# Keys of a cross-attention turned by transposing DMAs instead of TensorE transposes

## The chip, the cores and the metric

The kernel runs on one core of a Trainium2 chip. The metric is the device time of one execution in microseconds, as the median of several runs. The core has TensorE (PE: matmuls and transposes), VectorE (DVE), ScalarE (ACT), GpSimd (POOL) and the sync engine's queue (SP), which only issues DMAs. All DMAs of the core share 16 DMA engines.

## The reference

Eight sequences of 256 tokens with 1024 features go through one cross-attention with a residual and one gated feed-forward network with a residual. Only the first part is touched by the change.

```python
def xattn(text, features, Wq, bq, Wk, bk):      # text: layernorm(x), features: ctx_4096 (8, 256, 1024)
    Q = jnp.einsum('btx,dx->btd', text, Wq) + bq
    K = jnp.einsum('bpx,dx->bpd', features, Wk) + bk
    scores = jnp.einsum('btd,bpd->btp', Q, K) / sqrt(1024)
    return jnp.einsum('btp,bpd->btd', softmax(scores), features)

x = x + xattn(layernorm(x), ctx_4096, Wq, bq, Wk, bk)
x = x + ffn(layernorm(x), gate_q, gate_absmax, up_q, up_absmax, down_q, down_absmax)   # 4-bit weights, 1024 -> 3584 -> 1024
```

## The kernel before

A preparation of about 110 us forms the product `A` of the two weight matrices, so that the scores need only `x A ctx^T` and rows of biases. Then come eight steps, one per sequence ("batch" `b`, functions named `step(b)` on each engine), of about 37 to 41 us each. After them the feed-forward network runs for about 1500 us.

To keep precision, every operand is held as a pair of fp16 numbers, high and low ("hi" and "lo"); a product is three matmuls (`PARTS`: hi hi, hi lo, lo hi). "Keys" are the 256 rows of `ctx` of one sequence. They are needed in two forms: in rows (`keys16`, for the weighted sum at the end of attention) and turned, features in partitions (`keysT`, moving operand of the scores).

One step in the order of each engine's program, which is written out by hand:

- TensorE: eight blocks `o = 0..7` of 24 matmuls (L1533) that form `R = A^T x^T`; after block 1 the probabilities of the sequence before are turned (L1478); after blocks 4 to 7 one quarter of the keys is turned each (`turn_keys`, four fp32 transposes by the identity, L1470). Then the quarters of the next sequence's x (`turn_x`, also L1470) stand between the matmuls of the weighted sum of the sequence before (`attended`, L1494). Last come 48 matmuls of scores (L1569), in two halves of which the first is split 15 + 9 by the last `turn_x`. Each step begins by waiting until all four quarters of its x are split on VectorE (`s_xlo`, L1760).
- ScalarE: evicts each R block twice (L1662, L1664), makes the normalised x (L1612), scales the keys to fp16 hi rows and to fp32 rows (`keys_hi`, L1618 and L1619, after blocks 2 and 3), evicts each turned quarter of keys as hi (`turned_keys_hi`, L1624), and those of x (L1603).
- VectorE: scales, layernorm statistics of a sequence two steps back, `keys_lo` (L1784: turned keys minus their hi part), then `x_lo(b + 1, 0..2)` (L1760) with residuals between (L1824), `key_max(b + 1)` (L1765: largest key, once the keys of the next sequence have landed), `x_lo(b + 1, 3)`, and the softmax's maximum (L1798).
- GpSimd: R's low parts (L1423, one per block), the low parts of the key rows (L1427, after blocks 3 and 4; they raise `s_klo`), differences for a Strassen-like form of the feed-forward input (L1183 to L1191), and at the end of the step `reduce_max(b + 1)` (L1415, L1416), a maximum over partitions that waits for `key_max(b + 1)`.
- SP queue, in order: pieces of decoded weights and loads of packed weights where a table puts them (`units_due`, L301 and L284), a prefetch of x (L1370), x rows for the residual (L1380), turns of feed-forward input by transposing DMAs (`t_turn`, L1228) with the store of an earlier one (`t_store`, L1239), the load of the next sequence's keys (L1389; it waits for `s_klo` of this sequence since the buffer `keys` is single), and the store of y (L1358).

So keys run through a ring over two steps: load (L1389), `key_max` on VectorE, `reduce_max` on GpSimd, `keys_hi` on ScalarE, key low parts on GpSimd, and then the load of the next keys.

## Time and profile before

| what | value |
|---|---|
| median of 3 runs | 1978.07 us (1976.69 to 1984.44) |
| span of the profiled execution, first to last instruction | 1973.9 us; no whole time of its own is given for it, and the median of the runs lies 4.2 us above the span |
| PE, DVE, ACT, POOL busy over the span | 98%, 83%, 75%, 20% |
| attention steps b = 1 to 7 | 152.77 to 420.20 us |
| DMA queue of SP: share of the 16 engines over the span | 35.2% |

"Busy" is the time in which an engine's instruction ran. A wait is put down to the instruction that released it. The granted clock is TensorE's, as a part of full speed. A DMA's landing is counted from the start of its issue.

### The profile page before, as it was taken

How to read it: one execution, taken by the hardware profiler on the slowest of the kernel's cores; microseconds unless marked ns; L12 is line 12 of the kernel's file. 1: busy time of each engine (PE TensorE's matmuls, PEld its weight loads, DVE VectorE, ACT ScalarE, POOL GpSimd, SP SyncE). 2: the span in 40 equal slices, each digit the busy share in tenths (PEclk: the TensorE clock that was granted, in tenths of full speed). 3: DMA queues.
4: the chain of work that ended last, by engine and by line, in shares of the span. 5: the costliest groups of instructions: out<-in, count | busy, mean ns of one | idle time of the engine just before them, and what ended most of it. 6: DMA issues, size and time to landing. Idle time of an engine off the chain costs nothing.

```text
span 1973.9 us, 29877 instructions
## 1 busy us (share of the span) xinstructions
PE 1928.0 (98%) x9872; PEld 983.3 (50%) x9872; DVE 1637.0 (83%) x2758; ACT 1484.2 (75%) x2758; POOL 404.3 (20%) x600
## 2 busy tenths in 40 slices
PE   8989999989999999999999999999999999999999
PEld 3468878754444444444444444444444444444444
DVE  6757888986988988988988998898898898996963
ACT  3767886757889889889889889889899999900000
POOL 0022464441211211211211211111123222201110
PEclk9999999999999999999999999999999999999999
DMA  9112689683555555554544644645569899893562
GB/s 346 30 49 65 170 233 233 180 299 72 140 127 119 148 125 124 148 130 113 156 122 117 156 127 113 150 129 120 137 176 239 230 216 247 217 274 117 173 224 85
DMA packets 393626, 314.63 MB, mean 159 GB/s; under 512 B 327296, under 2 KB 327296, under 8 KB 391552
## 3 DMA queue, kind: packets, MB, share of 16 engines
q1 hardware_dynamic: 347360, 159.07, 35.2%
q0 software_dynamic: 44032, 153.65, 23.9%
q8 instruction: 78, 1.28, 0.3%
q14 instruction: 76, 0.62, 0.1%
q10 hardware_dynamic: 2080, 0.01, 0.1%
HBM read 154.31 MB, written 82.31 MB: 120 GB/s over the span
## 4 chain that ended last, share of the span: by engine, by line
PE 53%; ACT 22%; DVE 12%; issue 6%; DMA 1%; DVEq 0%; ACTq 0%; POOL 0%
PE ps L2125 38%; PE ps L2167 12%; ACT sq L346 7%; ACT sq L342 5%; ACT w L346 2%; DVE w L362 2%; ACT w L342 2%; PE ps L1494 1%; ACT halves L414 1%; PE ps L1569 1%; DVE tail L2277 1%; ACT tail L2198 1%; ACT T L1664 1%; PE ps L1533 1%; DVE tail L1219 1%
## 5 line engine op out<-in xcount | busy, mean ns | idle before, releaser
L2125 PE MATMUL ps<-T,wS 128*128 128x512 f16 x4704 | 1017.6, 379 | 4.1 <-DVE ps L2232 2.5
L2125 PEld LDWEIGHTS ps<-T,wS 128*128 128x128 f16 x4704 | 459.8, 98 | 558.4 <-issue 4.9
L346 ACT ACTIVATE sq<-sq 128x512 f32<-128x512 f32 x898 | 516.2, 627 | 0.0
L362 DVE SCALAR_TENSOR_TENSOR w<-sq,w 128x512 f32<-128x512 f32 x590 | 417.3, 707 | 109.5 <-ACT sq L346 99.6
L342 ACT ACTIVATE sq<-q 128x512 f32<-128x512 int32 x598 | 362.9, 631 | 49.6 <-DVE w L362 47.5
L2167 PE MATMUL ps<-T,tail 128*128 128x512 f16 x1584 | 345.0, 379 | 5.3 <-issue 2.1
L2167 PEld LDWEIGHTS ps<-T,tail 128*128 128x128 f16 x1584 | 154.6, 98 | 193.3 <-issue 5.9
L1533 PE MATMUL ps<-T 128*128 128x256 f16 x1536 | 174.1, 273 | 4.2 <-DVE T L1760 4.1
L2167 PE MATMUL ps<-T,wS 128*128 128x512 f16 x768 | 168.5, 379 | 1.0 <-DMA T<-halves 1.0
L430 DVE SCALAR_TENSOR_TENSOR halves<-w,halves 128x512 f16<-128x512 f32 x240 | 162.4, 686 | 6.4 <-ACT halves L414 6.2
L2073 POOL DMA_DIRECT2D keep_h<-tail x196 | 106.3, 542 | 295.7 <-DVE tail L2277 293.6
L1533 PEld LDWEIGHTS ps<-T 128*128 128x128 f16 x1536 | 149.8, 98 | 22.7 <-DVE T L1760 5.8
L414 ACT CAST halves<-w 128x512 f16<-128x512 f32 x204 | 126.0, 619 | 42.3 <-DVE w L362 32.2
L2277 DVE SCALAR_TENSOR_TENSOR tail<-tail 128x512 f16<-128x512 f32 x196 | 133.9, 683 | 10.4 <-ACT tail L2213 10.2
L2213 ACT CAST tail<-tail 128x512 f16<-128x512 f32 x196 | 119.6, 611 | 5.5 <-DVE tail L2246 5.5
L2167 PEld LDWEIGHTS ps<-T,wS 128*128 128x128 f16 x768 | 74.9, 98 | 92.1 <-DMA T<-halves 1.5
L284 POOL DMA_DIRECT2D q<-in_L_ffn_up_q x52 | 28.0, 538 | 353.0 <-DVE w L362 257.7
L287 POOL DMA_DIRECT2D q<-in_L_ffn_down_q x56 | 42.5, 760 | 227.0 <-DVE w L362 122.4
L2246 DVE SCALAR_TENSOR_TENSOR tail<-ps,up_out,tail 128x512 f32<-128x512 f32 x112 | 83.6, 746 | 2.1 <-PE ps L2125 1.1
L2198 ACT ACTIVATE tail<-ps,gate_out 128x512 f32<-128x512 f32 x112 | 76.0, 678 | 6.1 <-DVE ps L2236 3.7
L399 DVE TENSOR_TENSOR w<-w 128x512 f32<-128x512 f32 x112 | 78.1, 717 | 1.3
L1423 POOL TENSOR_TENSOR T<-tail,T 128x256 f16<-128x256 f32 x64 | 55.1, 870 | 95.8 <-ACT T L1664 53.6
(226 smaller groups left out, 1936.8 us busy)
## 6 DMA issues: line engine op xcount, KB each, us to landing
keep_h<-tail POOLq DMA_DIRECT2D x196, 256.0 KB, 2.5
tail<-keep_h POOLq DMA_DIRECT2D x66, 512.0 KB, 5.0
wS<-keep_h POOLq DMA_DIRECT2D x32, 512.0 KB, 4.8
q<-in_L_ffn_down_q POOLq DMA_DIRECT2D x56, 256.0 KB, 4.2
q<-in_L_ffn_up_q POOLq DMA_DIRECT2D x52, 256.0 KB, 2.9
q<-in_L_ffn_gate_q POOLq DMA_DIRECT2D x48, 256.0 KB, 3.4
keep_x<-T SPq DMA_DIRECT2D x38, 256.0 KB, 3.2
T<-in_x SPq DMA_DIRECT2D x9, 1024.0 KB, 5.6
```

What stands on the lines that cost most here:

```text
L342: nc.scalar.activation(place, un.q[:, ring, :], ACT.Square, bias=b, scale=a).then_inc(un.s_act, 1)
L346: nc.scalar.activation(place, place, ACT.Square, bias=b, scale=a).then_inc(un.s_act, 1)
L362: nc.vector.scalar_tensor_tensor(out=out, in0=square_place(un, u, i - 1), scalar=FACTORS[i - 1][1], in1=un.w[:, buf, :], op0=ALU.add, op1= ...
L414: nc.scalar.copy(un.halves[:, z % HALF_RING, 0, :], source_of(un, t, z)).then_inc(un.s_whi, 1)
L430: nc.vector.scalar_tensor_tensor(out=un.halves[:, z % HALF_RING, 1, :], in0=source_of(un, t, z), scalar=1.0, in1=un.halves[:, z % HALF_RIN ...
L1533: last = nc.tensor.matmul(r_bank(o), t.A[:, a, k, o * P:(o + 1) * P], xnT[:, c, k, :], start=k == 0 and j == 0, stop=k == KT - 1 and j == ...
L2073: nc.gpsimd.dma_start(t.hs[form, pair, :, side, :], t.hst[:, n % HST_RING].rearrange("p a d -> p (a d)")).then_inc(s_hst[n % HST_RING], 16)
L2125: last = nc.tensor.matmul(ps[:, bank, :], un.wS[:, z % SLOTS, a, kt, :], t.Tp[side][product][:, :, b, kt, :], start=fresh and n == 0, stop ...
L2167: last = nc.tensor.matmul(ps[:, j, :], h[:, j // PAIRS, a, tok], quad(q, c)[:, b].rearrange("p k d -> p (k d)"), start=fresh and n == 0, s ...
L2198: nc.scalar.activation(t.act_buf[e], ps[:, EVICT_BANK[product] + side, :], ACT.Silu, scale=t.gate_out[:, 2 * pair + row:2 * pair + row + 1 ...
L2213: nc.scalar.copy(t.hst[:, n % HST_RING, 0, :], t.act_buf[2 * FORM_BUF[form] + side]).then_inc(s_hhi, 1)
L2277: nc.vector.scalar_tensor_tensor(out=t.hst[:, n % HST_RING, 1, :], in0=t.act_buf[2 * FORM_BUF[form] + side], scalar=1.0, in1=t.hst[:, n % ...
```

## The change

The four quarters of turned keys no longer pass TensorE, ScalarE and VectorE. Instead the SP queue issues four transposing DMAs per sequence, two from the hi rows and two from the lo rows in `keys16`, straight into `keysT`, whose layout becomes `a i k m` (row tile before feature tile). They stand in SP's program after `units_due(base + 4)` and before the load of x rows for the residual. `s_kev` and `s_ktlo` go; TensorE waits for `s_kturned` ahead of the scores. The transposes of x now wait for `s_xlo` alone, and the load of the next keys waits only for `s_klo`. GpSimd's instructions stay as they are.

```diff
-        t.keysT = big(40, 8).rearrange("p (a k t) -> p a k t", a=2, k=KT)
+        t.keysT = big(40, 8).rearrange("p (a i k m) -> p a i k m", a=2, i=TB, k=KT)
...
+        def turn_keys(b, part):
+
+            sp.wait_ge(s_klo if part else s_khi, TB * (b + 1))
+            if part == 0:
+                wait(sp, s_scores, TB * b)
+            for i in range(TB):
+                sp.dma_start(keysT[:, part, i, :, :], keys16[:, b % 2, part, i, :], transpose=True).then_inc(s_kturned, 16)
...
             units_due(base + 3, base + 4)
+            turn_keys(b, 0)
+            turn_keys(b, 1)
             if b >= 2:
...
-                sp.wait_ge(s_t, 2 * XG * (b + 1))
                 sp.wait_ge(s_klo, TB * (b + 1))
                 sp.dma_start(keys[:, :, :], t.ctx_t[b + 1]).then_inc(s_keys, 16)
...
-            if b > 0 and g >= 2:
+            if b > 0:
                 pe.wait_ge(s_xlo, XG * b + g - 1)
-            elif b > 0:
-                pe.wait_ge(s_ktlo, XG * b + g - 1)
             turn(x_bank(b, g), x_group(b, g)[0])
-
-        def turn_keys(b, g):
-
-            if g % HALVES == 0:
-                pe.wait_ge(s_khi, TB * b + g // HALVES + 1)
-            if g < 2:
-                pe.wait_ge(s_xlo, XG * b + XG + g - 1)
-            else:
-                pe.wait_ge(s_ktlo, XG * b + g - 1)
-            turn(g % 2, keys[:, g // HALVES, g % HALVES * BANK:(g % HALVES + 1) * BANK])
...
-                if o in KEYS_AT:
-                    turn_keys(b, o - KEYS_AT[0])
...
-            pe.wait_ge(s_ktlo, XG * (b + 1))
+            pe.wait_ge(s_kturned, 16 * 2 * TB * (b + 1))
...
-                        last = nc.tensor.matmul(score_bank(i), RT[:, a, k, i * P:(i + 1) * P], keysT[:, c, k, :],
+                        last = nc.tensor.matmul(score_bank(i), RT[:, a, k, i * P:(i + 1) * P], keysT[:, c, :, k, :],
...
-        def turned_keys_hi(b, g):
-            i, h = g // HALVES, g % HALVES
-            act.wait_ge(s_t, 2 * XG * b + XG + g + 1)
-            nc.scalar.copy(keysT[:, 0, 4 * h:4 * h + 4, i * P:(i + 1) * P],
-                           ps[:, g % 2, :].rearrange("p (k t) -> p k t", k=4)).then_inc(s_kev, 1)
...
-        def keys_lo(b, g):
-            i, h = g // HALVES, g % HALVES
-            dve.wait_ge(s_kev, XG * b + g + 1)
-            if g == XG - 1:
-
-                dve.wait_ge(s_klo, TB * (b + 1))
-            nc.vector.tensor_tensor(keysT[:, 1, 4 * h:4 * h + 4, i * P:(i + 1) * P],
-                                    ps[:, g % 2, :].rearrange("p (k t) -> p k t", k=4),
-                                    keysT[:, 0, 4 * h:4 * h + 4, i * P:(i + 1) * P], ALU.subtract).then_inc(s_ktlo, 1)
```

The SP queue in step b = 4 stands so before, from the prefetch of x to the load of the next keys (T is the large buffer that holds x rows, keys and turned pieces; `keep_x` is in HBM):

```order
L1370 DMA T<-in_x 128x2x1024
L1380 DMA T<-in_x 128x2x1024
L1228 DMA_TRANSPOSE T<-tail 128x8x128
L1239 DMA keep_x<-T 128x1024
L1389 DMA T<-in_ctx 128x2x1024
```

and so now:

```order
L1377 DMA T<-in_x 128x2x1024
L1361 DMA_TRANSPOSE T<-T 128x8x128 x4
L1389 DMA T<-in_x 128x2x1024
L1228 DMA_TRANSPOSE T<-tail 128x8x128
L1239 DMA keep_x<-T 128x1024
L1397 DMA T<-in_ctx 128x2x1024
```

Four transposing DMAs came in behind the prefetch and ahead of three DMAs and the load of the next keys; the third of the four waits for `s_klo`, as the load of keys does.

TensorE's program in one step before, from the first two R blocks to the first part of the scores (`ident,T` are key quarters, `ident,tail` x quarters or probabilities):

```order
L1533 MATMUL ps<-T 128x256 x48
L1478 MATMUL ps<-ident,tail 128x128 x4
L1533 MATMUL ps<-T 128x256 x72
L1470 MATMUL ps<-ident,T 128x128 x4
L1533 MATMUL ps<-T 128x256 x24
L1470 MATMUL ps<-ident,T 128x128 x4
L1533 MATMUL ps<-T 128x256 x24
L1470 MATMUL ps<-ident,T 128x128 x4
L1533 MATMUL ps<-T 128x256 x24
L1470 MATMUL ps<-ident,T 128x128 x4
L1470 MATMUL ps<-ident,tail 128x128 x4
L1494 MATMUL ps<-T,tail 128x512 x12
```

and now:

```order
L1529 MATMUL ps<-T 128x256 x48
L1486 MATMUL ps<-ident,tail 128x128 x4
L1529 MATMUL ps<-T 128x256 x144
L1478 MATMUL ps<-ident,tail 128x128 x4
L1502 MATMUL ps<-T,tail 128x512 x12
```

The sixteen fp32 transposes of keys are gone, and nothing else moved on TensorE.

## Rows read from the trace of the kernel before

**Rows 1.** Windows, step b = 4 and all steps: us, PE, PEld, DVE, ACT, POOL, clock, DMA, GB/s
```profile
265.35:302.30 36.95, 35.87 (x302) 29.66 (x301) 31.96 (x73) 27.23 (x47) 18.59 (x16) 1.00 0.98 237
...
119.80:420.20 300.40, 282.58 (x2342) 233.94 (x2340) 244.94 (x508) 227.10 (x400) 131.16 (x123) 0.98 0.62 167
```

**Rows 2.** Waits of PE from 130 to 430 us, the largest: total, times, longest
```profile
PE ps L1470 <- DVE T L1784: 9.9, 9, 3.2
```

**Rows 3.** Timeline of PE in step b = 4: start, us, line, operation, count
```profile
278.89 0.60 PE L1470 MATMUL ps<-ident,T 128*128 128x128 f32 x4
279.33 2.78 PE L1533 MATMUL ps<-T 128*128 128x256 f16 x24
281.95 0.60 PE L1470 MATMUL ps<-ident,T 128*128 128x128 f32 x4
```

**Rows 4.** Timeline of DVE: the largest key of sequences 3 to 7
```profile
225.50 2.27 DVE L1765 TENSOR_REDUCE kmax<-T 128x1 f32<-128x2048 f32 x1
...
262.40 2.29 DVE L1765 TENSOR_REDUCE kmax<-T 128x1 f32<-128x2048 f32 x1
...
299.37 2.27 DVE L1765 TENSOR_REDUCE kmax<-T 128x1 f32<-128x2048 f32 x1
...
336.44 2.27 DVE L1765 TENSOR_REDUCE kmax<-T 128x1 f32<-128x2048 f32 x1
...
376.16 2.27 DVE L1765 TENSOR_REDUCE kmax<-T 128x1 f32<-128x2048 f32 x1
```

**Rows 5.** Timeline of POOL: steps 0 and 4, the last row of step 7
```profile
134.21 2.13 POOL L1427 TENSOR_TENSOR T<-T 128x1024 f16<-128x1024 f32 x1
...
264.77 0.19 POOL L1415 TENSOR_TENSOR spare<-kmax 128x1 f32<-128x1 f32 x1 [4.99 <-DVE kmax L1765]
271.21 0.38 POOL L1416 PARTITION_ALL_REDUCE kall<-kmax  x1 [6.25 <-issue]
278.75 3.58 POOL L1423 TENSOR_TENSOR T<-tail,T 128x256 f16<-128x256 f32 x4 [7.16 <-issue]
...
286.00 2.13 POOL L1427 TENSOR_TENSOR T<-T 128x1024 f16<-128x1024 f32 x1
...
396.98 2.14 POOL L1427 TENSOR_TENSOR T<-T 128x1024 f16<-128x1024 f32 x1
```

**Rows 6.** Timeline of the SP queue in step b = 4: issue start, us
```profile
286.68 0.38 SPq L1380 DMA_DIRECT2D T<-in_x  x1
289.39 1.24 SPq L1228 DMA_TRANSPOSE T<-tail  x1
...
291.34 0.39 SPq L1389 DMA_DIRECT2D T<-in_ctx  x1
```

**Rows 7.** Landing us: x rows and keys of step 4, then all seven key loads
```profile
T<-in_x SPq DMA_DIRECT2D x1, 1024.0 KB, 4.9
...
T<-in_ctx SPq DMA_DIRECT2D x1, 1024.0 KB, 7.8
...
DMA to landing us min/median/max: 4.8/5.4/7.8
```

**Rows 8.** DMAs from 460 to 560 us: SP's queue share, its transposes and landing
```profile
q1 hardware_dynamic: 20694, 5.36, 29.4%
...
wS<-halves SPq DMA_TRANSPOSE x19, 3.3
```

**Rows 9.** Timeline of PE: scores of step 0, starts of steps 1 and 2
```profile
144.56 3.41 PE L1569 MATMUL ps<-T 128*128 128x256 f16 x15
...
152.77 5.40 PE L1533 MATMUL ps<-T 128*128 128x256 f16 x48
...
191.03 5.40 PE L1533 MATMUL ps<-T 128*128 128x256 f16 x48
```

**Rows 10.** Timeline of PE in step 7, last longest wait and the rows behind
```profile
409.20 1.11 PE L1264 MATMUL ps<-ident,tail 128*128 128x128 f32 x4 [2.95 <-DVE T L1784]
410.10 3.98 PE L1494 MATMUL ps<-T,tail 128*128 128x512 f16 x12
```

More of the change, by code:

```diff
@@ L1303, in attend @@
     s_xf, s_keys = sem("s_xf"), sem("s_keys")
-    s_kmax, s_kall, s_kin, s_khi, s_klo, s_ktlo, s_rlo, s_ptlo, s_out = (
-        sem(n) for n in ("s_kmax", "s_kall", "s_kin", "s_khi", "s_klo", "s_ktlo", "s_rlo", "s_ptlo", "s_attout"))
-    s_xn, s_dot, s_t, s_xhi, s_xlo, s_kev, s_r, s_rev, s_scores, s_neg, s_probs = (
-        sem(n) for n in ("s_xn", "s_dot", "s_t", "s_xhi", "s_xlo", "s_kev", "s_r", "s_rev", "s_scores", "s_neg", "s_probs"))
+    s_kmax, s_kall, s_kin, s_khi, s_klo, s_kturned, s_rlo, s_ptlo, s_out = (
+        sem(n) for n in ("s_kmax", "s_kall", "s_kin", "s_khi", "s_klo", "s_kturned", "s_rlo", "s_ptlo", "s_attout"))
+    s_xn, s_dot, s_t, s_xhi, s_xlo, s_r, s_rev, s_scores, s_neg, s_probs = (
+        sem(n) for n in ("s_xn", "s_dot", "s_t", "s_xhi", "s_xlo", "s_r", "s_rev", "s_scores", "s_neg", "s_probs"))
     s_pt, s_ptev, s_att, s_y, s_bn, s_bias, s_self = (
@@ L1316, in attend @@
     PROBS_AT = 1
-    KEYS_AT = range(4, 4 + XG)
     LAST = BATCH - 1
@@ L1377, in step @@
                 else:
-                    sp.wait_ge(s_t, 2 * XG * b + XG)
+                    sp.wait_ge(s_t, XG * (b + 1))
                     sp.wait_ge(s_dot, TB * BATCH)
@@ L1444, in gpsimd @@
         t_load(nc, pool, t, 0, 6)
-        pool.wait_ge(s_t, 2 * XG * BATCH)
+        pool.wait_ge(s_klo, TB * BATCH)
         pool.wait_ge(t.s_store, 16 * (LAST - 1))
@@ L1542, in step @@
             else:
-                pe.wait_ge(s_ktlo, XG * b + XG - 1)
                 late_turn(nc, pe, t, 0)
@@ L1550, in step @@
             else:
-                pe.wait_ge(s_ktlo, XG * BATCH)
                 late_turn(nc, pe, t, 1)
@@ L1601, in x_hi @@
         def x_hi(b, g):
-            act.wait_ge(s_t, 2 * XG * b + g + 1)
+            act.wait_ge(s_t, XG * b + g + 1)
             nc.scalar.copy(x_group(b, g)[1][0], ps[:, x_bank(b, g), :].rearrange("p (k t) -> p k t", k=4)).then_inc(s_xhi, 1)
@@ L1608, in x_normalise @@
                 act.wait_ge(s_xf, 16 * (b - 3))
-            act.wait_ge(s_t, 2 * XG * (b - 1) + HALVES * (i + 1))
+            act.wait_ge(s_t, XG * (b - 1) + HALVES * (i + 1))
             act.wait_ge(s_dot, TB * b)
@@ L1635, in late_places_due @@
             if m == 1:
-                act.wait_ge(s_t, 2 * XG * BATCH)
                 act.wait_ge(s_klo, TB * BATCH)
@@ L1665, in step @@
                                      bias=t.query_col[:, o:o + 1]).then_inc(s_rev, 1)
-                if o in KEYS_AT:
-                    turned_keys_hi(b, o - KEYS_AT[0])
                 if o in KEYS_HI_AT:
@@ L1852, in step @@
             for g in range(XG):
-                keys_lo(b, g)
                 if old and g >= 2:
```

## The prediction

> **What bounds the kernel now.** I read the windows by step first. In the attention TensorE works 282.6 of 300.4 us (94%), VectorE 82%, ScalarE 76%, and in step 4 the 16 DMA engines are busy 98% of the time [rows 1]. So the first candidate for the bound is TensorE, and the change takes work from it. The waits of TensorE show what else the key turns cost: 9.9 us in nine waits for `keys_lo` on VectorE (L1784) [rows 2], and 2.95 us in step 7 [rows 10].
>
> A sum of TensorE's work says that this is not the whole of it. A block of R is 24 matmuls and takes 281.95 - 279.33 = 2.62 us, a turned quarter 279.33 - 278.89 = 0.44 us [rows 3]. A step is eight blocks (21.0), nine quarters and probabilities (4.0), 48 score matmuls at the same 0.109 us (5.2) and 24 matmuls of 512 columns at twice that (5.2): 35.4 us. Step 4 lasts 36.95 [rows 1]. What holds the rest is the ring of the keys. I follow it through the timelines of four queues: the largest key of sequence 4 is begun on VectorE at 262.40 and ends at 264.7 [rows 4]. GpSimd starts at 264.77, its reduction over partitions stands between two stretches of 6 and 7 us without visible work, R's low parts follow at 278.75, and the second low part of the keys ends at 286.00 + 2.13 = 288.13 [rows 5]. SP issues the next keys at 291.34 [rows 6], they take 7.8 us to land [rows 7], that is 299.14, and the next largest key begins at 299.37 [rows 4]. The ring is closed with 0.2 us to spare: 25.73 on VectorE and GpSimd, then 11.24 for SP and the load, together 36.97. The reader is to see that the starts of L1765 at 262.40, 299.37 and 336.44 [rows 4] are 36.97 and 37.07 apart, the ring's length, and TensorE starts its step 2.95 us after each (265.35 against 262.40), since the last quarter of x is split behind the key maximum on VectorE. TensorE is nearly the bound, and the ring is the bound in steps 3 to 5.
>
> **What the change removes.** 16 fp32 transposes a step: 4 x 0.44 = 1.75 us of TensorE, 14 us in eight steps. 32 casts on ScalarE and 32 subtractions on VectorE go as well; I price them at nothing of their own, for those engines are 76% and 82% busy, but the waits for them are the 9.9 and 2.95 us above. Taken alone, these would be a gain of up to 14 + 12.9 = 27 us.
>
> **What it adds, and where.** Four transposing DMAs a step. A transpose costs SP 1.24 us to issue [rows 6] and lands 3.3 us after the start of issue. From 460 to 560 us 19 of them and one load used 29.4% of 100 us of all engines, so one costs at most 29.4 / 19 = 1.55 us of DMA engine time [rows 8]. The hi pair is issued when ScalarE has scaled the keys, in a stretch where SP only waited for the x rows; it costs nothing while that stretch is there. The lo pair starts with `s_klo`, at 288.13 + 0.1 in step 4's clock. Behind it on SP stand the x rows for the residual, one turn with its store, and then the keys of the next sequence. Before, the x rows and the turn had been issued at 286.68 and 289.39 [rows 6], mostly before or right after 288.13; now all wait. Counted from `s_klo`: two issues 2.6, x rows 0.4, turn to keys 1.95 (291.34 - 289.39), so the keys are issued at +5.05 instead of 291.34 - 288.13 = +3.2.
>
> The landing is the disputed price. The engines serve the queue in order. A 1 MB load lands in 4.9 us on a queue that is free [rows 7]; I take 1.1 of it before and 0.9 after the stream, so 3.0 us of engines, near what 3.3 - 1.55 leaves for a transpose's fixed part. The lo pair keeps the engines until +3.8, the x rows until +6.8, the turn until +8.35, its store (a quarter of a load) +9.1, the keys +12.1, landed at +13.0. The same arithmetic for step 4 before gives 297.0, and 299.14 was measured, 2.1 more; but that was the longest of seven landings, whose median is 5.4 [rows 7]. So +13.0 to +15.1; I take +13.6, near the lower end because of that median. The lower bound below these is the old 11.24, if the engines overlap the three transfers fully.
>
> On the queue: the Trainium skill, "DMA: Bandwidth & Descriptors", section "Queues, rings and completion order", says that each DMA engine takes the descriptors of one ring in ring order. By it the keys land behind the x rows, as the 7.8 us of [rows 7] suggest too, though no row here shows the order by itself. The same page, section "Latency and other measured facts", gives 261 GB/s for a DMA transpose with a non-contiguous middle dimension, which for 256 KB would be an estimate of 1.0 us, against at most 1.55 by the row; by the page's figure the keys would land 0.5 us sooner and the total come out some 2 us lower. The row is used here.
>
> So the ring becomes 25.7 + 13.6 = 39.3 us, against 36.97, while TensorE's own path falls to 33.6 us. The wait goes from `keys_lo` to the key load: TensorE will be late at the start of each step, on the last quarter of x.
>
> **The sum by steps.** Step 0: the lo part ends at 136.34 [rows 5], the second lo transpose is issued at 137.7 and lands at 141.0; I set the scores at 142 instead of 144.56 and, since those ran at a lower clock (15 matmuls in 3.41 us, twice the pace of the others) [rows 9], the start of step 1 between 2.5 and 5 us earlier: 4. Step 1 has no x rows, the keys are issued 2.6 us after `s_klo`, and TensorE gains 1.75 and two waits of the mean 1.1: step 2 starts 8 us earlier, at 183.0 instead of 191.03 [rows 9], and its key maximum at 180.0. From here the ring counts. Step 2 (no store ahead, 38.4): 218.4, 7.1 earlier than 225.50. Steps 3, 4, 5 at 39.3: 257.7, 297.0, 336.3, against 262.40, 299.37, 336.44 [rows 4]: the lead melts to 0.1. Step 6: GpSimd's part took 399.12 - 376.16 = 23.0 in step 7 [rows 4, 5] and 25.7 in step 4; with 24.4 the ring is 38.0, so 374.3 against 376.16, 1.9 earlier. In step 7 no key load follows. TensorE saves 1.75 us, the wait of 2.95, one of 0.6 and the slow matmuls behind it (3.98 against 2.75 us for twelve of 512 columns) [rows 10]: 6.5 us. Its new wait: low parts at 374.3 + 23.0 = 397.3, turned by 402.0, while TensorE reaches the scores at 374.3 + 2.95 + 27.9 = 405.1; no cost. End of attention: 8.4 us earlier. The feed-forward part follows it, since its first transfers of turned input also come from that end; its work is the same. Against the span of 1973.9 that is 1965.5, and with the 4.2 us around it, 1969.7: **1970 us**.
>
> **Rivals.** Gains over 0.5% mean less than 1968.2 us, losses over 0.5% more than 1988.0; half a per cent, 9.9 us, is about what a measurement of this kernel can tell from no change.
>
> - *Ring as forecast* (38 to 41 us): 1963 to 1979. Chance 0.55, of it about 0.12 under 1968.2. For it: four queues whose times close within 0.2 us.
> - *Ring unchanged in length* (keys land 11.2 after `s_klo` as before, since the x rows' transfer overlaps). Each of steps 3 to 5 stays at 36.97, step 6 at 35.6: lead 7 + 4 + 6.5 = 17.6, so 1960. For it: the load at 7.8 had a slow landing that need not recur. Against: 1.85 us later issue, one more load close ahead. Chance 0.15.
> - *TensorE bound*: each of steps 2 to 7 at 34.5; lead 8 + 229.2 - 207 = 30, so 1948. It needs a ring under 34.5; GpSimd's part alone is 25.7 and a free load 4.9 + 2.3. Chance 0.07.
> - *The other side, the DMA engines as the bound.* Step 4 has 98% DMA share already [rows 1], that is 36.2 us of engines; 4 x 1.55 more make 42.4. If the busy share is true work and not packets waiting, then hi and lo pairs land late, and steps 3 to 6 take 42 to 45 us. At 44: lead 7.1 - 3 x 7.0 - 4.3 + 6.5 = -11.7, so 1990. It decides for slower from a mean period of 43.5 us. For it: the 98%. Against: 237 GB/s in that step, where a transposing DMA or a load by itself reaches more, and the mean share over the attention is 62% [rows 1]. Chance 0.13.
> - *The change does nothing*: ScalarE and VectorE fill the holes with other waits and the ring takes all: 1978. Chance 0.10.
>
> **How the numbers follow.** Likeliest: 1970, its own range 1963 to 1979. Range for 8 in 10: 1957 to 1986, which leaves out TensorE bound and the worst of the DMA case. Faster: 0.12 + 0.15 + 0.07 = 0.34; slower: 0.11 of the DMA case and 0.02 elsewhere; same: 0.53.
>
> **What would show it.** In the changed profile: the starts of the key maximum about 39 us apart in steps 3 to 5, 38.4 before; VectorE idle ahead of it for a DMA of keys; TensorE waiting for x's last split at the start of steps 3 to 7, up to 5 us each; no wait of note ahead of the scores, where `s_kturned` stands; keys issued about 5 us after the end of the second low part and landing 8 to 9 us later; step 2 starting near 183; scores of step 7 near 405 instead of 414. Wrong would be: starts under 37.5 or over 42 apart, or a long wait of TensorE for the turned keys, which would mean that the transposes land later than 4.7 us after the low parts.

## The result, and the profile after

The changed kernel is slower by a third of a per cent: 1985.33 us median (1979.27 to 1993.6, 20 runs) against 1980.28 us (1967.45 to 1989.9, 20 runs), ratio 1.0033, 95% interval [1.0019, 1.0047]. A second measurement gave 1.0038 [1.0019, 1.0057]; one of its twelve runs was in a slower state (2008.87 us) and is left out of the ratio. The prediction was 1970, a small gain.

TensorE works less, and the steps are longer. Its windows for step b = 4 and for all steps, to be held against [rows 1]:

```profile
261.37:300.11 38.74, 35.25 (x285) 28.53 (x285) 31.44 (x69) 25.45 (x43) 18.54 (x16) 0.96 0.97 230
...
119.80:419.20 299.40, 270.93 (x2214) 222.59 (x2212) 222.81 (x470) 211.58 (x366) 133.88 (x119) 0.96 0.76 191
```

TensorE is busy 270.9 instead of 282.6 us, VectorE 222.8 instead of 244.9, ScalarE 211.6 instead of 227.1; DMA share rose from 0.62 to 0.76. The stretch is hardly shorter (299.4 against 300.4). The starts of the largest key on VectorE answer to [rows 4]; the bracket is the idle time ahead and what ended it:

```profile
219.18 2.29 DVE L1748 TENSOR_REDUCE kmax<-T 128x1 f32<-128x2048 f32 x1 [2.20 <-DMA T<-in_ctx]
258.42 2.29 DVE L1748 TENSOR_REDUCE kmax<-T 128x1 f32<-128x2048 f32 x1 [2.51 <-DMA T<-in_ctx]
297.17 2.29 DVE L1748 TENSOR_REDUCE kmax<-T 128x1 f32<-128x2048 f32 x1 [1.95 <-DMA T<-in_ctx]
338.29 2.29 DVE L1748 TENSOR_REDUCE kmax<-T 128x1 f32<-128x2048 f32 x1 [3.35 <-DMA T<-in_ctx]
378.37 2.29 DVE L1748 TENSOR_REDUCE kmax<-T 128x1 f32<-128x2048 f32 x1 [3.42 <-DMA T<-in_ctx]
```

Before, none of these rows had a bracket. They are now 39.2, 38.8, 41.1 and 40.1 us apart. That no row of before has a bracket says something of its own: VectorE came to the key maximum by its own work. Its last wait ahead of 299.37 in the kernel before, behind which it works 11.3 us without a gap, is this one:

```profile
288.07 0.69 DVE L1784 TENSOR_TENSOR T<-ps,T 128x512 f16<-128x512 f32 x1 [1.84 <-ACT T L1624]
```

The SP queue in step 4 (start, duration of the issue), against [rows 6]:

```profile
277.64 8.95 SPq L1361 DMA_TRANSPOSE T<-T  x4
286.68 0.53 SPq L1389 DMA_DIRECT2D T<-in_x  x1
287.31 1.23 SPq L1228 DMA_TRANSPOSE T<-tail  x1
288.59 0.57 SPq L1239 DMA_DIRECT2D keep_x<-T  x1
289.21 0.77 SPq L1397 DMA_DIRECT2D T<-in_ctx  x1
290.08 3.58 SPq L1228 DMA_TRANSPOSE T<-tail  x1
```

and GpSimd's second low part of the keys, after which the third transpose may go:

```profile
281.82 2.13 POOL L1435 TENSOR_TENSOR T<-T 128x1024 f16<-128x1024 f32 x1
```

It ends at 283.95; the keys are issued at 289.21, that is +5.26, where it was +3.2. The seven key loads land in 5.9/7.9/9.3 us (least, median, most), against 4.8/5.4/7.8 in [rows 7]:

```profile
L1397 SPq DMA_DIRECT2D T<-in_ctx x7: 477/581/771, 139.0 to 370.2; - x7
...
  DVE kmax L1748: 14.4, 7
...
DMA to landing us min/median/max: 5.9/7.9/9.3
```

TensorE feels it where a step starts, as its largest waits from 130 to 430 us say (total, times, longest):

```profile
PE ps L1529 <- DVE T L1743: 19.0, 6, 4.3
PE ps L1478 <- DVE T L1743: 8.3, 4, 3.5
```

L1743 is the split of x, of which the last quarter stands behind the key maximum. The waits for the turned keys of [rows 2] are gone; 27.3 us of other waits stand in their place.

The end of the attention, on TensorE. The first row is the start of step 7:

```profile
381.31 8.17 PE L1529 MATMUL ps<-T 128*128 128x256 f16 x48 [4.01 <-DVE T L1743]
...
412.89 0.63 PE L1264 MATMUL ps<-ident,tail 128*128 128x128 f32 x4 [1.20 <-DVE T L1279]
413.35 1.80 PE L1561 MATMUL ps<-T 128*128 128x256 f16 x15
...
425.35 8.31 PE L1502 MATMUL ps<-T,tail 128*128 128x512 f16 x24 [1.49 <-DVE tail L1763]
...
455.78 2.75 PE L2097 MATMUL ps<-T,wS 128*128 128x512 f16 x12 [0.85 <-DVE T L1279]
```

The scores of step 7 start 1.0 us earlier than before (414.35 in the trace of before), but the 48 matmuls of 256 columns took 8.17 us instead of 5.40 [rows 9], and 24 of 512 columns 8.31. A row of the feed-forward part that both traces have is 2.9 us later (before: 452.92). I call that last row "the mark" from here on.

### The profile page after: what moved, and what is told of

Same layout as the page of the kernel before. It is cut to its first block, busy times and chain, and to the rows that moved or that the text cites. A ratio compares the mean times of both kernels' runs of the same rounds, so it can differ in the third digit from the quotient of the medians.

```text
span 1981.5 us, 29563 instructions
## 1 busy us (share of the span) xinstructions
PE 1921.9 (97%) x9744; PEld 973.4 (49%) x9744; DVE 1617.0 (82%) x2726; ACT 1469.5 (74%) x2726; POOL 409.7 (21%) x600
## 4 chain that ended last, share of the span: by engine, by line
PE 54%; ACT 20%; DVE 8%; issue 6%; DMA 3%; POOL 2%; SPq 1%; DVEq 0%; ACTq 0%
PE ps L2097 38%; PE ps L2139 12%; ACT sq L346 7%; ACT sq L342 5%; PE ps L1529 3%; ACT w L346 2%; DMA T<-in_ctx 2%; ACT w L342 2%; DVE w L362 1%; POOL T L1435 1%; ACT halves L414 1%; POOL T L1431 1%; PE ps L1502 1%; DVE tail L2249 1%; DMA T<-halves 1%
## 5 line engine op out<-in xcount | busy, mean ns | idle before, releaser
L1529 PE MATMUL ps<-T 128*128 128x256 f16 x1536 | 178.3, 280 | 20.9 <-DVE T L1743 20.9
L430 DVE SCALAR_TENSOR_TENSOR halves<-w,halves 128x512 f16<-128x512 f32 x240 | 162.4, 686 | 6.9 <-ACT halves L414 6.7
```

The lines of the kernel that those rows point to most:

```text
L430: nc.vector.scalar_tensor_tensor(out=un.halves[:, z % HALF_RING, 1, :], in0=source_of(un, t, z), scalar=1.0, in1=un.halves[:, z % HALF_RIN ...
L1529: last = nc.tensor.matmul(r_bank(o), t.A[:, a, k, o * P:(o + 1) * P], xnT[:, c, k, :], start=k == 0 and j == 0, stop=k == KT - 1 and j == ...
```

## The experiments

Eighteen further runs: sixteen kernels made for this, the changed kernel again and e1 again. For each, "step" is the mean distance of the key maxima of sequences 3 to 7 (a quarter of the distance from the third to the seventh start), "scores" the start of the scores of step 7, "mark" as above, all from one profile; ratios are against runs of the kernel before on the same chip, whose median was 1977.0 to 1980.3 us, so kernels from different chips are best compared by their ratios. Of one and the same kernel two profiles differ by 0.3 us in "step" and about 2 us in "mark".

| kernel | step | scores | mark | median | ratio, 95% interval |
|---|---|---|---|---|---|
| before | 37.67 | 414.35 | 452.92 | 1980.28 | |
| after | 39.80 | 413.35 | 455.78 | 1985.33 | 1.0033 [1.0019, 1.0047] |
| r_after_again | 39.49 | 411.30 | 453.26 | 1986.59 | 1.0038 [1.0019, 1.0057] |
| e1 after, keys loaded first | 37.22 | 399.37 | 444.40 | 1971.54 | 0.9972 [0.9949, 0.9995] |
| r_e1_again | 37.53 | 399.89 | 442.72 | 1977.91 | 0.9985 [0.9962, 1.0007] |
| e2 before, keys loaded first | 37.13 | 410.35 | 450.47 | 1981.45 | 1.0006 [0.9983, 1.0029] |
| e3 after, no key turns | 37.50 | 402.42 | 443.51 | 1974.39 | 0.997 [0.9949, 0.9991] |
| e4 after, TensorE kept busy | 39.93 | 413.95 | 457.60 | 1990.83 | 1.0059 [1.0038, 1.0081] |
| e5 e1 + piece 1 later | 37.28 | 399.63 | 441.92 | 1974.52 | 0.9974 [0.9951, 0.9997] |
| e6 before + piece 1 later | 38.15 | 408.95 | 452.25 | 1978.14 | 1.0009 [0.999, 1.0028] |
| e7 after + piece 1 later | 40.23 | 415.57 | 461.52 | 1983.29 | 1.0032 [1.0009, 1.0054] |
| e8 e1 + x3 first | 38.82 | 410.62 | 452.33 | 1982.66 | 1.0018 [1.0002, 1.0035] |
| e9 e5 + x3 first | 37.43 | 402.77 | 445.31 | 1974.91 | 0.9973 [0.996, 0.9987] |
| e10 after + x3 first | 39.22 | 412.60 | 454.48 | 1986.76 | 1.0041 [1.0025, 1.0058] |
| e11 before + x3 first | 37.55 | 410.18 | 451.69 | 1981.54 | 1.0001 [0.9984, 1.0018] |
| e12 e9, less VectorE | 35.97 | 393.42 | 436.20 | 1966.43 | 0.9943 [0.9919, 0.9967] |
| e13 e9, more ScalarE | 37.75 | 402.52 | 444.61 | 1979.38 | 1.0005 [0.9987, 1.0023] |
| e14 before, less VectorE | 36.61 | 401.64 | 442.19 | 1973.18 | 0.997 [0.9951, 0.999] |
| e15 after, less VectorE | 39.64 | 411.75 | 457.90 | 1990.94 | 1.0061 [1.0038, 1.0085] |
| e16 e2, less VectorE | 35.70 | 399.17 | 438.84 | 1970.72 | 0.996 [0.9937, 0.9983] |

**The place of the key load (e1, e2).** In the changed kernel the load moves from behind the x rows and the turn to directly behind the lo pair:

```diff
             turn_keys(b, 1)
+            if b < LAST:
+                sp.dma_start(keys[:, :, :], t.ctx_t[b + 1]).then_inc(s_keys, 16)
             if b >= 2:
```

> The changed kernel, only the load of the next keys is issued directly behind the two transposes of the low parts, ahead of the x rows and the turn of feed-forward input. Ring theory (the key load stands too late in SP's queue, and its landing sets the next key maximum): the load is issued 2.7 us after the second low part instead of 5.3, lands 5.5 to 6.5 us later instead of 8 to 9, the ring falls from about 39 us to 34.5, TensorE becomes the bound, starts of the key maximum 34.5 to 36 us apart in steps 3 to 6; total 1958 to 1968 us, 17 to 27 below the changed kernel. DMA theory (the 16 engines have too much work, whatever the order): starts stay 38.5 to 41 us apart, total 1983 to 1988. Clock theory (lower granted clock behind waits of TensorE is what the change costs): the waits at the starts of steps go, so 5 to 8 us below the changed kernel, about 1978.

> The kernel before, only the load of the next keys is issued ahead of the x rows and the turn of feed-forward input, as soon as the last quarter of keys is turned and the low parts are made. It measures the order alone, without the change. Ring theory: the ring of 36.97 us had 0.2 us to spare, so it falls to about 33, and TensorE's path with its waits for the subtraction of turned keys remains, 35.4 + about 1: starts of the key maximum 36 to 36.6 us apart in steps 3 to 5, total 2 to 6 us below before, 1974 to 1978. If the order gives as much here as in the changed kernel with the same move (over 15 us), then the key turns by DMA have no part in the gain. DMA theory: no change, 1980.

e1 waits for its keys once (0.71 us) instead of seven times. Its key loads in step 4, on the SP queue:

```profile
273.52 8.93 SPq L1361 DMA_TRANSPOSE T<-T  x4
282.50 0.58 SPq L1383 DMA_DIRECT2D T<-in_ctx  x1
283.18 0.43 SPq L1392 DMA_DIRECT2D T<-in_x  x1
```

The steps fall by 2.0 to 2.6 us and the two medians by 0.4 to 0.7% against the changed kernel's; neither interval of e1 meets one of the changed kernel. So the late load was what made the changed kernel slower. In the kernel before, the same move does nothing that can be told, as the 11.3 us of VectorE without a gap would have it. And e1's steps stop at 37 us (34.5 to 36 were expected, and 1958 to 1968 us in all) although nothing waits for the keys any more: that is not what the prediction's account of [rows 4] lets one expect, and the later runs are about it.

**Without the key turns, and with TensorE kept busy (e3, e4).** e3 issues the four transposes for sequence 0 alone, so that all scores but its own use wrong keys; e4 puts 26 matmuls, read by nobody, ahead of each of the steps 3 to 7.

```diff
-            turn_keys(b, 0)
-            turn_keys(b, 1)
+            if b == 0:
+                turn_keys(b, 0)
+                turn_keys(b, 1)
```

```diff
+            if b >= 3:
+                pe.wait_ge(s_xlo, XG * (b + 1) - 1)
+                for _ in range(26):
+                    nc.tensor.matmul(ps[:, 0, 0:SEQ], t.A[:, 0, 0, 0:P], t.A[:, 0, 0, 0:SEQ], start=True, stop=True)
             pe.wait_ge(s_xlo, XG * (b + 1))
```

> The changed kernel without its transposing DMAs from the second sequence on: the scores of all sequences use the turned keys of the first one. So the work taken off TensorE, ScalarE and VectorE is gone, and nothing is added to the DMA engines or to SP's queue. Ring theory: the key load goes back to about 3 to 3.5 us after the low parts and lands as before, so the starts of the key maximum stay 36 to 37 us apart in steps 3 to 5 though TensorE has only 33.6 us of work; attention ends 8 to 14 us earlier than before, total 1966 to 1972. If TensorE had been the bound: 34 to 35 us apart, total 1950 to 1957. The difference to the changed kernel is the price of the DMAs: about 14 to 18 us by the ring theory.

> The changed kernel with 26 matmuls of 256 columns, whose result nobody reads, issued by TensorE at the starts of steps 3 to 7, where it waits 2.9 to 4.3 us for the last quarter of x. Clock theory: the 48 matmuls behind the wait, which took 6.7 to 8.2 us instead of 5.4 in four of these five steps, take 5.4; only step 7 and the stretch behind it stand on the path, so the scores of step 7 start 2.7 us earlier, and the total falls by 3 to 6 us to about 1980. Ring theory alone: the starts of the key maximum stay 39 to 41 us apart in steps 3 to 6, and the total stays within 1 us of the changed kernel.

With the transposes away and the old order, VectorE no longer waits for keys from step 1 on, and the steps are 37.5 us; with e1, which issues all four and has 37.2, it was their place ahead of the load that hurt. In e4 the first 48 matmuls of four of the five steps are back at 5.4 us (7.08 in step 4), and the kernel is no faster (1.0059, where about 1980 us were expected if the clock was the cost); the low clock behind the waits is a companion of the ring, not a cause of its length.

**GpSimd's differences (e5, e6, e7).** In e1 ScalarE idles 2.69 us and VectorE 1.81 us for turned input piece 1, whose difference GpSimd computes. The three kernels move ScalarE's `t_hi(c, 1)` and VectorE's `t_lo(c, 1)` behind the first quarter of x (ScalarE's part is shown):

```diff
-                if old and o in (6, 7):
-                    t_hi(nc, act, t, c, o - 6)
+                if old and o == 6:
+                    t_hi(nc, act, t, c, 0)
...
+                if old and g == 0:
+                    t_hi(nc, act, t, c, 1)
```

> The kernel of e1_keys_load_first, in which ScalarE's high part and VectorE's low part of turned input piece 1 stand behind the first quarter of the next x instead of ahead of it. In e1 the steps stay 37 us although VectorE never waits for the keys after step 1. Second-ring theory: what closes in 37 us is the way from the key maximum over GpSimd (reduction, low parts, the first difference) to ScalarE's idle time of 2.7 us and VectorE's of 1.8 us for that piece, and from there through the x splits to the next key maximum. Then the starts of the key maximum in steps 3 to 6 come 35.0 to 36.2 us apart instead of 37.2, the scores of step 7 start near 395 (e1: 399.4), and the time is about 1968 against 1971.5. Rival, the key load is the only ring: e1 has taken it out, so the 37 us come from the work on TensorE and its low clock; the starts stay at 37.2 and the time at 1971.5.

> The kernel before with the same move of piece 1 and nothing else. If two rings of nearly the same length bind there, taking one out gives nothing: starts of the key maximum 36.7 to 37.5 apart, time 1978 to 1982, and a wait of VectorE for the key load appears. If the ring over the differences was the only one that bound, the starts come 36 apart and the time is 1975 or less.

> The changed kernel with the same move of piece 1, the key load still late on the queue. Theory that the late key load sets its steps of 39 to 41 us: starts of the key maximum stay 38.5 to 41 apart, VectorE's wait for the keys grows from 14 us to 18 or more, and the time is that of the changed kernel, 1983 to 1987. Rival, that the differences set it: starts 37 to 38 apart and 1978 or less.

> The changed kernel once more, for a second profile: starts of the key maximum again 38.5 to 41 apart, and the wait near 1737 us for the decoded down weights, 3.8 us in the first profile against 1.0 before, anywhere from 1 to 6 us, since other kernels of this study had 2.4 to 5.4 there. If it is again 3.5 to 4.5 it belongs to the change.

The second-ring theory, as the only one, falls: e5's steps are those of e1. The two waits for piece 1 are gone, but VectorE's work did not shrink. In step 4 of e1 the low parts of pieces 0 to 2 and L430 took 1.34, 1.72, 0.68 and 1.15 us, in e5 1.48, 1.78, 1.69 and 1.76, since two of them now run beside GpSimd's work: 1.82 us more, just what the wait had been. e6 gains nothing either: its steps of 38.15 us are longer than before, and VectorE waits for the keys once (1.03 us). e7 keeps the long steps, and VectorE's wait for the keys grows from 14.4 to 17.6 us, as the late load would have it.

**The last quarter of x ahead of the key maximum (e8 to e11).** ScalarE's part of that quarter likewise goes ahead of turned input piece 4.

```diff
-                key_max(b + 1)
                 x_lo(b + 1, 3)
+                key_max(b + 1)
```

> The kernel of e1_keys_load_first, in which VectorE splits the last quarter of the next x ahead of the key maximum (and ScalarE's part of it stands ahead of turned input piece 4, which waits for a DMA). Third theory, after e5 showed that the wait for the differences is not the bound: TensorE's step start waits for one chain, seven R blocks on TensorE, then 15 us of work in a row on VectorE, in which the key maximum of 2.3 us stands ahead of the last quarter. Then TensorE's step starts come 1.0 to 2.3 us closer together (e1: 36.7 to 37.5 apart in steps 3 to 6), if the wait for the differences does not stand in the way: about 36, and the time is 1965 to 1970. Rival, GpSimd's chain from the key maximum binds: the maximum is 0.7 us later, steps of 37.5 to 38, time 1973 or more.

> The kernel of e5 (keys loaded first, piece 1 later) with the same move of the last quarter of x ahead of the key maximum. Third theory: the steps of 36.7 us fall to 34.5 to 35.7, the scores of step 7 start near 391 to 395, TensorE's waits at step starts fall from 2 us to under 0.5, and the time is 1962 to 1968. Rival, VectorE's own work (34.6 us in a step of 37.15 of e5) or GpSimd's chain binds: steps stay at 36.5 or above and the time is 1971 to 1975.

> The changed kernel with only the move of the last quarter of x ahead of the key maximum; the key load is still late on the queue. TensorE then no longer waits behind the late key load at the start of a step. If the ring of the keys sets the changed kernel's steps, they stay 38.5 to 41 us long all the same, and TensorE's waits move from the step start to the scores or to the turns: time 1981 to 1988. If only the place of the key maximum ahead of the last quarter made the late load hurt, the steps fall to 37 or less and the time to 1976 or less.

> The kernel before with the same move. The ring of the keys, with 0.2 us to spare, gets 0.7 us longer; TensorE's own work there is 35.4 us in a step of 37. If the key ring alone binds: starts of the key maximum 37.0 to 37.8 apart, time 1976 to 1984. If the chain through VectorE to the last quarter bound as well, which e6 and e2 could not tell: steps of 36 us and the time under 1975.

No gain over e1 or e5 came, and e10 and e11 stay where the changed kernel and the kernel before were. e8 went to the rival's side, and its step 4 shows why: kernel e8, GpSimd, ScalarE, VectorE and TensorE, start, duration, idle time ahead.

```profile
259.61 0.57 POOL L1422 TENSOR_TENSOR spare<-kmax 128x1 f32<-128x1 f32 x1 [5.54 <-DVE kmax L1749]
...
284.48 1.71 POOL L1183 TENSOR_TENSOR tail<-tail 128x512 f32<-128x512 f32 x1
...
286.23 0.62 ACT L1212 CAST tail<-tail 128x512 f16<-128x512 f32 x1 [3.84 <-POOL tail L1183]
...
286.88 1.72 DVE L1219 SCALAR_TENSOR_TENSOR tail<-tail 128x512 f16<-128x512 f32 x1 [1.81 <-ACT tail L1212]
...
290.42 1.09 PE L1477 MATMUL ps<-ident,tail 128*128 128x128 f32 x4 [4.19 <-DVE T L1744]
...
296.22 0.69 DVE L1744 TENSOR_TENSOR T<-ps,T 128x512 f16<-128x512 f32 x1 [1.51 <-ACT T L1594]
296.82 2.28 DVE L1749 TENSOR_REDUCE kmax<-T 128x1 f32<-128x2048 f32 x1
```

From the key maximum (257.26) over GpSimd's reduction, the difference, ScalarE and VectorE back to the next one it is 39.6 us: the second ring does exist. Its last part passes TensorE as well: TensorE's third turn of x had waited 4.19 us for VectorE's first split, 15 matmuls of scores behind it took 3.41 us instead of 1.80, and VectorE then waited 1.51 us for the last quarter. e9 differs from e8 only by the move of piece 1, and its steps are 1.4 us shorter, its median 7.8 us lower. But in e9 something else stops the steps at 37.4. VectorE in its step 4:

```profile
280.12 2.00 DVE L1219 SCALAR_TENSOR_TENSOR tail<-tail 128x512 f16<-128x512 f32 x1 [4.51 <-ACT tail L1212]
282.04 1.15 DVE L362 SCALAR_TENSOR_TENSOR w<-sq,w 128x512 f32<-128x512 f32 x1
283.12 1.75 DVE L430 SCALAR_TENSOR_TENSOR halves<-w,halves 128x512 f16<-128x512 f32 x1
284.80 0.68 DVE L1746 TENSOR_TENSOR T<-ps,T 128x512 f16<-128x512 f32 x1
285.40 1.78 DVE L1219 SCALAR_TENSOR_TENSOR tail<-tail 128x512 f16<-128x512 f32 x1
287.10 1.39 DVE L1800 SCALAR_TENSOR_TENSOR T<-ps,rsum,T 128x512 f32<-128x512 f32 x2
288.42 0.67 DVE L1746 TENSOR_TENSOR T<-ps,T 128x512 f16<-128x512 f32 x1
289.02 1.69 DVE L1219 SCALAR_TENSOR_TENSOR tail<-tail 128x512 f16<-128x512 f32 x1
290.63 1.40 DVE L1800 SCALAR_TENSOR_TENSOR T<-ps,rsum,T 128x512 f32<-128x512 f32 x2
291.95 1.27 DVE L1746 TENSOR_TENSOR T<-ps,T 128x512 f16<-128x512 f32 x2
293.15 2.27 DVE L1751 TENSOR_REDUCE kmax<-T 128x1 f32<-128x2048 f32 x1
```

Behind a wait of 4.51 us for ScalarE come 13.0 us without a gap, all of it ahead of the key maximum. This too is part of a ring: ScalarE's cast that ended the wait (L1212, 279.42) stands behind its eviction of TensorE's seventh block, and TensorE, which had begun step 4 at 256.18, begins the next at 293.31, 0.1 us behind the last split of x. That is 37.1 us over TensorE, ScalarE and VectorE.

**VectorE's part and ScalarE's part (e12 to e16).** Four kernels leave the residual's sum out but for 2 of 512 columns in steps 1 to 7, with the same waits and signals; e13 adds three evictions on ScalarE instead.

```diff
             tile = y_rows(t, b)[:, i, h * BANK:(h + 1) * BANK]
+            source = att_bank(b, n)
+            if b < LAST:
+                tile, source = tile[:, 0:2], source[:, 0:2]
```

```diff
+                if 2 <= b < LAST and o < 3:
+                    nc.scalar.activation(extra[:, o, :], r_bank(o), ACT.Identity, scale=t.a_out[:, 0:1],
+                                         bias=t.query_col[:, o:o + 1])
```

> The kernel of e9_all_three, in which the residual's four instructions on VectorE work on 2 of 512 columns in steps 1 to 7 (the residual is left out but for these; waits and signals are the same). That takes 4 x 0.6 = 2.4 us from the 13 us that VectorE works without a gap ahead of the key maximum. ScalarE-VectorE ring: the key maxima come 34.8 to 35.8 us apart instead of 37.2, the scores of step 7 start near 394 instead of 402.8, and the time is 1963 to 1969. Rival, GpSimd's chain or the key load sets the steps: they stay over 36.5 and the time at 1973 to 1976.

> The kernel of e9_all_three with three more evictions of 256 columns on ScalarE (0.45 us each, into a buffer that nobody reads) behind the first three R blocks of steps 2 to 6. ScalarE-VectorE ring: 1.35 us more in each of five steps, key maxima 38.3 to 38.8 apart, the scores of step 7 about 6.7 us later, the time 1979 to 1983. Rival: ScalarE is 75% busy and waits up to 4 us a step for a DMA, so the work is hidden: steps and time as in e9, 1973 to 1977.

> The kernel before with the same residual left out but for 2 columns. Ring of the keys alone, closed with 0.2 us to spare: key maxima stay 36.6 to 37.3 apart in steps 3 to 5, VectorE now waits 1 to 2.4 us for the key load ahead of each, and the time is 1976 to 1980. If VectorE's part was what bound: 35 to 36 apart and under 1972.

> The kernel of e2 (the kernel before with its key load ahead of the x rows and the turn) with the same residual left out but for 2 columns: both rings are shorter. If the two together held the kernel before at 37 us, the key maxima come 35.2 to 36.2 apart here and the time is 1966 to 1973; TensorE's own 35.4 us a step, with its key turns, would then be the bound. If they stay at 37, the transposes of the keys and their waits bound it and neither ring did.

> The changed kernel with the residual on VectorE left out but for 2 of 512 columns in steps 1 to 7, 2.4 us less of VectorE's work in a step. If the ring of the keys binds: the key maxima stay 38.3 to 41 apart from the second on, VectorE's wait for the key load grows from 14 us in all to 20 or more, and the time is 1981 to 1987. If VectorE's work binds there too, as it did in the kernel before by 1.5 us a step: 37.5 or less and under 1978.

> The kernel of e1_keys_load_first once more. If its gain over the kernel before is real, the ratio is again 0.995 to 0.9985; if it was chance, 0.999 to 1.002. Key maxima 36 to 38 apart with no wait for the key load after the first.

The residual's four instructions took 2.79 us in step 4 of e9 and 0.67 us in e12, so 2.1 us went, where I had counted 2.4. With the keys in time that shortens the step by 1.5 (e9 to e12) and 1.4 us (e2 to e16). In the kernel before (e14) it is 1.1 in the mean, but nearly all of it in one place: the distances of sequences 3 to 6 fall only from 36.98 to 36.71 us, with VectorE now waiting 0.97 us for the key load in step 4, and the last one from 39.72 to 36.28. By the time alone e14 (0.997) and e16 (0.996) can't be told apart. In the changed kernel they shorten nothing (39.64 against 39.80 and 39.49), and the wait for the keys takes them up. Kernel e15, VectorE, 130 to 430 us:

```profile
DVE kmax L1748 <- DMA T<-in_ctx: 20.7, 7, 4.4
```

14.4 became 20.7. Its time, 1.0061 of the kernel before, lies above the 1981 to 1987 us expected of it; why is open. e13 is a miss: of 1.35 us added on ScalarE 0.3 came out in the step. VectorE's wait ahead of the stretch grew to 5.89 us in step 4, but its first instruction then took 1.25 us instead of 2.00, since it no longer met GpSimd's low part. So the stretch on VectorE binds, ScalarE ahead of it only in part. The median of e13 is 4.5 us above e9's (6 us by the ratios, since the chips differ) with the scores and the mark where they were in e9, so that rise is not from the attention.

## Why the prediction was wrong

*What held.* The keys pass VectorE, GpSimd, SP and the load in one ring, and the change makes it longer. From the key maximum at 258.42 to the end of the low parts 25.5 us (I took 25.7), the issue at +5.26 (5.05), the keys there at +13.2 (13.6), together 38.75 (39.3). Up to step 4 the key maxima stand where they were forecast: 180.52, 219.18, 258.42 and 297.17 against 180.0, 218.4, 257.7 and 297.0. The wait moved from the turned keys to x's last split, and TensorE never waits for `s_kturned`. The DMA engines were not the bound: the steps with DMA shares of 0.97 to 1.01 were set by the wait for one load, and e1 moves the same bytes in steps 2 to 2.6 us shorter (two of them, of 37.0 and 36.7 us, show shares of 1.08 and 1.04).

*The step that failed* is the sum's last part: "so 374.3 against 376.16" and "In step 7 ... 6.5 us", hence "End of attention: 8.4 us earlier". The 6.5 us that TensorE was to save in step 7 did not arrive at all: from the key maximum of sequence 7 to the mark it is 76.8 us in the kernel before, and 77.4 and 76.6 us in the two profiles of the changed one. In detail:

- The ring was sized too short. Steps 5 and 6 were sized 39.3 and 38.0; they are 41.1 and 40.1. Step 5 is 26.5 to the end of the low parts, 5.3 to the issue and 9.3 for the load, where 25.7, 5.05 and 8.55 stood; step 6 is 25.6, 6.3 and 8.2 where 24.4, 5.05 and 8.55 stood. No one piece is far off; the 24.4 leaned on the single short step 7 of before, and SP's issues ran longer than I allowed. Key maximum of step 7: 378.37, not 374.3. That is 4.1 us (376.71 and 2.4 us in the second profile).
- TensorE was taken as the only engine on the way from there to the scores. They start 35.0 us after the key maximum (34.6 in the second profile; 38.2 before), not 30.8. It waits there for VectorE's split of a turned input piece (L1279), a path that the prediction has no term for. These are the end of step 7 in the second profile, on TensorE, and VectorE's first L1279 in the second profile, the first profile and the kernel before:

```profile
379.65 5.41 PE L1529 MATMUL ps<-T 128*128 128x256 f16 x48 [1.80 <-DVE T L1743]
...
410.60 0.91 PE L1264 MATMUL ps<-ident,tail 128*128 128x128 f32 x4 [3.33 <-DVE T L1279]
411.30 3.23 PE L1561 MATMUL ps<-T 128*128 128x256 f16 x15
```

```profile
409.78 0.68 DVE L1279 TENSOR_TENSOR T<-ps,T 128x512 f16<-128x512 f32 x1
```

```profile
412.06 0.68 DVE L1279 TENSOR_TENSOR T<-ps,T 128x512 f16<-128x512 f32 x1
```

```profile
410.27 0.68 DVE L1279 TENSOR_TENSOR T<-ps,T 128x512 f16<-128x512 f32 x1
```

That instruction starts 33.1, 33.7 and 34.1 us after the key maximum, though TensorE's part differs by several us. The slow 48 matmuls of the first profile (2.8 us) are not what cost the time: in the second profile and in e4 they take 5.4 us, the wait for VectorE is then 3.3 instead of 1.2 us, and the scores stand 34.6 and 34.4 us behind the key maximum.
- "The feed-forward part follows it" was taken as one to one. From the scores to the mark it is 38.6 us in the kernel before and 42.4 and 42.0 in the changed one. The first profile shows a wait of 1.2 us for ScalarE and 24 matmuls in 8.31 us where they took 5.5; the second has neither, but other waits in their place (0.9 for GpSimd, 1.5 for VectorE) and 15 slow matmuls of scores. So no single one of them is the cause, and which chain sets the mark was not isolated. e1 shows the same at a larger scale: 15.0 us earlier at the scores, 8.5 at the mark.

Two readings of the prediction were off by themselves. Its scores at 405.1 are 9.2 us earlier than before, its end of attention 8.4, though both come from the same sum. And a transposing DMA of 256 KB in at most 1.55 us is shown by [rows 8] to reach 169 GB/s at least, which does not bear out "more" than the 237 GB/s of the step.

*The rest.* The changed kernel is 5.1 us slower by its median in the first measurement and 9.6 in the second (6.5 and 7.5 by the ratios). The mark is only 2.9 us late in the one profile and 0.3 in the other. Nearly all that remains lies behind 1490 us, where waits for decoded weights vary between executions. TensorE's waits in the last stretch, first of the changed kernel, then of its second profile, then of e11, the kernel before but for the place of x's last quarter:

```profile
PE ps L2139 <- DMA T<-halves: 3.8, 1, 3.8
PE ps L2139 <- DVE tail L2297: 1.8, 1, 1.8
```

```profile
PE ps L2139 <- DVE tail L2291: 5.2, 1, 5.2
PE ps L2139 <- DMA T<-halves: 4.6, 1, 4.6
```

```profile
PE ps L2169 <- DMA T<-halves: 6.8, 1, 6.8
PE ps L2169 <- DVE tail L2327: 1.7, 1, 1.7
```

They add up to 3.4 in the kernel before and to between 2 and 15 in the others, of either kind. Whether the change shifts their mean by some 3 us stays open; one profile a kernel can't tell.

*What the prediction did not see* decides what the change could have brought. It took the 36.97 us of the kernel before for the ring of the keys alone. But two more chains close in nearly the same time: GpSimd's differences over ScalarE to VectorE (seen in e8), and TensorE's seven blocks over ScalarE to VectorE's stretch ahead of the key maximum (11.3 us in the kernel before, 13.0 in e9). In the kernel before, shortening the first or the second alone, or moving the last quarter of x, gives nothing (e2, e6, e11); taking work from VectorE alone gives 0.3% (e14), though little of it in steps 3 to 5. With the key load and VectorE's stretch both relieved, the kernel before comes to 35.70 us a step (e16), near the 35.4 of TensorE's own work that the prediction had summed, and the changed one, with more moved, to 35.97 (e12), where TensorE's own work is 33.6. So the rival "TensorE bound" (34.5) needed not only a short key ring but a lighter VectorE, and even with both it was not reached; what holds e12 at 36 was not looked for. The 14 + 12.9 us that the change takes off TensorE were mostly not there to be had. The early lead was real: step 2 starts at 183.46 instead of 191.03, 7.6 us earlier, before any ring was full.

The kernels that compute the whole and are faster than the kernel before are those with the change and the key load first: e1 (0.9972 and 0.9985), e5 (0.9974) and e9 (0.9973). Three of the four intervals end below 1. A gain of 0.15 to 0.3% over the kernel before is likely; over the changed kernel it is clear.

## What to carry to other kernels

A wait that is nearly closed in a trace names one ring, not the only one: before you count work off the critical path as gain, sum each engine's ungapped stretch between two handovers of the same period, and ask which of them closes within a microsecond of it. New DMAs that wait for a signal belong behind every load that has been waiting for the same signal; here the same four transposes cost 0.3% ahead of the load's neighbours and nothing once the load stood right behind them. A second profile of the same kernel is worth its price: waits and slow matmuls that looked like causes in the first were absent in the second, with the same length of the whole. And a lead at the end of a stage is only as good as the next stage's first wait: follow it to a row that both traces have.

## What the runs showed of the hardware

- Issue time is not fixed. A transposing DMA takes SP 1.23 us to issue when little stands ahead, and 3.58 us right behind a key load of 1 MB (the rows of the SP queue above). So a transposing DMA behind a large load held the queue up to 2.35 us longer.
- Four transposing DMAs raised the landing of the next load from a median of 5.4 to 7.9 us. With the load right behind them (e1) it was 5.8: the x rows and the turn in front made most of the difference.
- VectorE's instructions with both operands in SBUF took 1.69 to 2.00 us while GpSimd worked (L1219 in e9) and 0.68 us otherwise (the same line at 259.32 in e5); those that read PSUM (L1746, L1800 by the piece) stayed at 0.68 us and 0.70 us beside the same GpSimd work. By these rows a move of such an instruction into GpSimd's idle time would save about 1 us (an estimate; no run made it), and e5 lost 1.8 us by moves the other way.
- Behind TensorE waits of 3.5 to 4.3 us, at the starts of steps 3, 4, 6 and 7, the next 48 matmuls took 6.7 to 8.2 us instead of 5.4; behind 2.87 us at the start of step 5 they took 5.41, but in the second profile 7.08 behind 2.65. The granted clock over these steps was 0.93 to 0.98, where step 4 of the kernel before has 1.00: for part of the time the engine ran at 1.2 instead of 2.4 GHz.
